# Linear attention and a mixture of experts on one core: the first group's experts woven into the last two rounds of the attention

## The chip, the cores and the metric

The kernel runs on one core of one Trainium2 chip. The metric is the device time of one execution in microseconds (us). The median of three runs stands beside the range of the three.

## What is computed

The input `x` is 4 sequences of 512 tokens with 256 features. Two layers follow, each added to its input and layer-normalised.

```python
x = _layernorm(x + attn(x))     # gated delta rule: 16 key heads, 32 value heads of 128
x = _layernorm(x + ffn(x))

def attn(x):
    mixed = silu(causal_conv(x @ w_qkv, conv_w))      # 4 taps
    q, k, v = split(mixed); z = x @ w_z
    beta = sigmoid(x @ w_b)
    g = -exp(A_log) * softplus(x @ w_a + dt_bias)
    # for each token: S = S*exp(g); S += k (v - k.S)*beta; o = q.S
    return (rmsnorm(o * silu(z)) * norm_gamma) @ w_out

def ffn(x):                      # 8 experts, the best 2 of each token, one shared expert
    h = rmsnorm(x) * rms_weight
    top 2 of softmax(h @ router_w), weights normalised to sum 1
    return sum_e w_e * (silu(h @ w_gate[e]) * (h @ w_up[e])) @ w_down[e] + shared(h)
```

## The kernel before

**Attention.** The work is cut into 64 bodies (16 key heads by 4 sequences; `n` counts them, 0 to 63). A body has 8 cells: 4 chunks of 128 tokens for each of 2 value heads. Within a body the delta rule is solved by blocks: products of the keys (`products`), decays by a scan (`scan`, `m`, `p`), the inverse of a triangular matrix by doubling (steps `join`, `growx`, `growt` at levels 0 to 5, then `newton`, `res`, `finish`, `tt`), and then a recurrence over the 4 chunks: `solve` (TensorE, L1013) -> `u` (ScalarE) -> `write` (TensorE, L1023) -> `s` (VectorE, the new state) -> `read` (TensorE, L1001) -> `rhs` (VectorE) -> the next `solve`. The outputs (`out`, L1039 and L1040) are gated (`og`, VectorE, L1246), squared (`power`, ScalarE), raised to -1/2 and applied (`pow`, `ogs`, GpSimd, L871, L876 and L880), transposed (`turn`, TensorE, L1046) and projected (`project`, L1055) into the accumulator `acc`.

**What sets the order.** There is no scheduler. The table `ORDER` lists for each engine the steps of one round, with the body that each belongs to: in round k a step with ahead 0, 1 or 2 works on body k, k+1 or k+2. `rounds` runs k from -2 to 63 and leaves out bodies that do not exist, so rounds 62 and 63 lack the projections, convolutions and scans of later bodies. Every engine runs its own list strictly in order; semaphores join them. SyncE's queue issues all loads and stores in order.

**Gates.** Before the rounds, and between the first steps of round -2, the decays and betas of all bodies are made in `gates_vector`, `gates_scalar`, `decays_scalar`, `decays_tensor`. GpSimd meanwhile fills the tile `N` with six copies of the identity (`fill_n`, L780). `gall` (VectorE, L335) is what the three matmuls L409 wait for. `decays_scalar` takes exponentials, copies the two row tiles (L374) that are stored to DRAM and loaded back by all bodies, and takes three more exponentials (L377); then ScalarE loads the table for Silu and runs `silu` (L1093) and the second `tap` (L1080).

**Experts.** 4 groups (one sequence each) of 9 experts (8 routed, one shared), i = 0 to 35 in all. For each expert TensorE does `into` (two halves; 8 records of 512 columns in the trace, L527), ScalarE a Silu (L598), VectorE the product `gated` (L678), TensorE `outof` (8 records of 256 columns, L565), VectorE `added` (L692). Before a group's experts come its steps, numbered k: 0 (VectorE, residual and statistics, L623 to L611), 1 (GpSimd, a power, L503), 2 (VectorE, normalise, L615), 3 (ScalarE, squares), 4, 5 (a power, L506), 6 (VectorE, scale), 7 (TensorE transposes L541, ScalarE copies), 8 (TensorE, router logits L548; VectorE, top 2), 9 (a power, L510), 10 (VectorE, weights). For group 0 they stand in round 63 by the table `PREPARE`; for the later groups between experts by `AFTER_EXPERT`. The expert weights are loaded once (`s_mw`) over the attention's `xT`, `conv` and `w_kh`; `into` 1 is followed by `outof` 0, and so on, one expert behind.

```python
for name, i, n in rounds(ORDER["tensor"]):
    run(name, i, n)
    if n == BODIES - 1:
        for k in PREPARE["tensor"].get((name, i), ()):
            prepare_tensor(pe, k, 0)
moe_tensor(pe)
```

## Time and profile before

| | us |
|---|---|
| median of 3 runs | 2387.56 (2385.25 to 2388.07) |
| the profiled execution | 2386.43 |
| its span, first to last instruction | 2384.7 |
| TensorE busy in it | 2324.8 (97%) |
| VectorE, ScalarE, GpSimd busy | 1973.6, 1327.8, 1179.1 |
| mean granted TensorE clock | 0.988 of full speed |

The profiled execution took 1.13 us less than the median; 1.7 us of it lie outside its span. Busy time says how long an engine worked, not whether it was waited for. A timeline row gives the start, the time and the group of instructions; the bracket gives the idle time of the engine before it and what ended it.

### The profile page before, as it was taken

How to read it: one execution, taken by the hardware profiler on the slowest of the kernel's cores; microseconds unless marked ns; L12 is line 12 of the kernel's file. 1: busy time of each engine (PE TensorE's matmuls, PEld its weight loads, DVE VectorE, ACT ScalarE, POOL GpSimd, SP SyncE). 2: the span in 40 equal slices, each digit the busy share in tenths (PEclk: the TensorE clock that was granted, in tenths of full speed). 3: DMA queues.
4: the chain of work that ended last, by engine and by line, in shares of the span. 5: the costliest groups of instructions: out<-in, count | busy, mean ns of one | idle time of the engine just before them, and what ended most of it. 6: DMA issues, size and time to landing. Idle time of an engine off the chain costs nothing.

```text
span 2384.7 us, 53886 instructions
## 1 busy us (share of the span) xinstructions
PE 2324.8 (97%) x20046; PEld 1777.4 (75%) x20046; DVE 1973.6 (83%) x3426; ACT 1327.8 (56%) x4125; POOL 1179.1 (49%) x1198
## 2 busy tenths in 40 slices
PE   6899999999999999999999999999999999987998
PEld 3677877777777777777778777777777777775665
DVE  5888888888888888888888888888888888864665
ACT  3565556665556665566655566665566655652110
POOL 3465555555555555555655655555555555541000
PEclk8999999999999999999999999999999999998999
DMA  4011100111111111011111111111010110010000
GB/s 136 28 54 37 48 34 37 45 37 54 36 46 36 47 37 55 29 36 46 37 55 37 46 37 46 37 54 37 28 54 28 54 37 29 27 70 18 18 10 18
DMA packets 32099, 98.46 MB, mean 41 GB/s; under 512 B 4320, under 2 KB 9824, under 8 KB 31584
## 3 DMA queue, kind: packets, MB, share of 16 engines
q1 hardware_dynamic: 31840, 95.02, 11.3%
q8 instruction: 161, 2.64, 0.5%
q14 instruction: 98, 0.80, 0.1%
HBM read 92.39 MB, written 2.62 MB: 40 GB/s over the span
## 4 chain that ended last, share of the span: by engine, by line
PE 76%; POOL 11%; issue 8%; DVE 3%; ACT 1%; POOLq 0%; DMA 0%; SPq 0%; DVEq 0%; ACTq 0%
PE bank L915 15%; PE bank L939 8%; PE bank L1055 8%; PE bank L952 5%; PE bank L527 4%; PE bank L1013 4%; PE bank L1040 4%; PE bank L962 3%; PE bank L972 3%; PE bank L1001 3%; PE bank L1023 3%; PE bank L1039 3%; PE bank L1046 2%; PE bank L565 2%; PE bank L978 2%
## 5 line engine op out<-in xcount | busy, mean ns | idle before, releaser
L1173 DVE SCALAR_TENSOR_TENSOR conv<-bank,cw_all,conv 128x511 f32<-128x511 f32 (+2 forms) x768 | 565.9, 744 | 16.4 <-ACT conv L1080 7.2
L915 PE MATMUL bank<-xT,w_kh 128*128 128x512 f32 x1024 | 548.5, 618 | 2.3 <-ACT sqj L1102 2.3
L1209 DVE TENSOR_TENSOR N<-bank,lev 128x512 f16<-128x512 f32 x384 | 261.9, 682 | 163.5 <-PE bank L962 163.5
L844 POOL TENSOR_SCALAR_AFFINE_SELECT mhiT<-m32T 128x512 f16<-128x512 f32 x128 | 78.9, 638 | 490.3 <-DVE m32T L1185 490.3
L1125 ACT ACTIVATE X<-bank 128x512 f16<-128x512 f32 x384 | 227.9, 594 | 162.7 <-PE bank L972 157.3
L1080 ACT ACTIVATE conv<-bank,cw_all 128x512 f32<-128x512 f32 x256 | 176.0, 687 | 206.1 <-PE bank L915 206.1
L1055 PE MATMUL bank<-wo,ogT 128*128 128x256 f32 x1024 | 279.8, 396 | 0.0
L939 PE MATMUL bank<-w_kh,xT 128*128 128x256 f32 x1024 | 271.5, 388 | 0.5 <-ACT vals L1115 0.5
L1121 ACT ACTIVATE zs<-bank 128x512 f32<-128x512 f32 x128 | 76.5, 597 | 288.3 <-PE bank L939 288.3
L972 PEld LDWEIGHTS bank<-N,XT 128*128 128x128 f16 x3072 | 122.9, 98 | 127.9 <-DVE N L1209 109.3
L871 POOL TENSOR_TENSOR ms<-ms,epsq 128x8 f32<-128x8 f32 x64 | 12.7, 199 | 406.5 <-ACT og L1140 406.5
L1040 PE MATMUL bank<-U,pT 128*128 128x128 f32 x1024 | 188.8, 277 | 0.0
L939 PEld LDWEIGHTS bank<-w_kh,xT 128*128 128x128 f32 x1024 | 176.1, 192 | 14.8 <-ACT vals L1115 0.7
L962 PEld LDWEIGHTS bank<-X,mhiT 128*128 128x128 f16 x3072 | 137.7, 98 | 66.3 <-issue 20.9
L1055 PEld LDWEIGHTS bank<-wo,ogT 128*128 128x128 f32 x1024 | 176.4, 192 | 13.7
L915 PEld LDWEIGHTS bank<-xT,w_kh 128*128 128x128 f32 x1024 | 155.4, 191 | 17.8 <-ACT sqj L1102 4.0
L972 PE MATMUL bank<-N,XT 128*128 128x64 f16 x3072 | 155.1, 193 | 6.7 <-DVE N L1209 6.7
L1179 DVE TENSOR_TENSOR_SCAN decb<-egb,decb 128x512 f32<-128x512 f32 x128 | 155.6, 1216 | 5.6 <-POOL decb L822 5.6
L1040 PEld LDWEIGHTS bank<-U,pT 128*128 128x128 f32 x1024 | 156.7, 193 | 3.4
L1203 DVE STREAM_TRANSPOSE XT<-X 128x1024 f16<-128x1024 f16 x128 | 158.0, 1235 | 0.7 <-ACT X L1125 0.7
L1140 ACT ACTIVATE og<-og 128x128 f32<-128x128 f32 x512 | 151.0, 298 | 10.9 <-DVE og L1246 5.4
L962 PE MATMUL bank<-X,mhiT 128*128 128x64 f16 x3072 | 154.1, 193 | 2.7 <-ACT X L1125 2.1
(163 smaller groups left out, 5605.1 us busy)
## 6 DMA issues: line engine op xcount, KB each, us to landing
egb<-rows SPq DMA_DIRECT2D x64, 512.0 KB, 3.7
ecb<-rows SPq DMA_DIRECT2D x64, 512.0 KB, 3.7
w_kh<-w_heads SPq DMA_DIRECT2D x16, 768.0 KB, 6.0
wo_raw<-w_out SPq DMA_DIRECT2D x16, 256.0 KB, 6.3
xT<-x_cols SPq DMA_DIRECT2D x4, 512.0 KB, 5.6
qT<-x_rows SPq DMA_DIRECT2D x4, 512.0 KB, 3.5
xT<-gate_up SPq DMA_DIRECT2D x1, 2048.0 KB, 8.1
out<-og SPq DMA_DIRECT2D x4, 512.0 KB, 2.9
```

Of the source, the lines that this page charges most:

```text
L915: mm = pe.matmul(PB[j % 2][:, :], w[:, k, g * P:(g + 1) * P], xT[:, k, b * SEQ:(b + 1) * SEQ], start=(k == 0), stop=(k == KT - 1))
L939: mm = pe.matmul(PB[h][:, 256 * c:256 * c + 256], xT[:, k, t * P:(t + 1) * P], w[:, k, 512:768], start=(k == 0), stop=(k == KT - 1))
L962: mm = pe.matmul(IB[1 - i % 2][:, x * 64:(x + 1) * 64], mhiT[:, x, :], blocks(X[:, x:x + 1, :], i, 0), start=True, stop=True)
L972: mm = pe.matmul(IB[i % 2][:, x * 64:(x + 1) * 64], XT[:, x, :], blocks(N[:, i, x:x + 1, :], i, 0), start=True, stop=True)
L1040: mm = pe.matmul(dst, pT[:, p, x, :], U[:, x, :], start=(c == 0), stop=True)
L1055: mm = pe.matmul(OB[h][:, 256 * c:256 * c + 256], ogT[:, 2 * i + v, :], wo[:, head % 2, v, :], start=(v == 0), stop=(v == VH - 1))
L1080: act.activation(conv[:, g, :], PB[i % 2][:, :], ACT.Copy, scale=cw_all[:, head, g * TAPS + 3:g * TAPS + 4]).then_inc(s_tap, 1)
L1125: act.activation(blocks(X[:, :, :], i, 0), packed(IB[i % 2], i), ACT.Copy).then_inc(s_x, 1)
L1173: dve.scalar_tensor_tensor(conv[:, g, m:], PB[j % 2][:, 0:SEQ - m], cw_all[:, head, g * TAPS + 3 - m:g * TAPS + 4 - m], conv[:, g, m:], op ...
L1179: dve.tensor_tensor_scan(d, egb[:, p, 512 * i:512 * i + 512], d, 0.0, ALU.mult, ALU.add).then_inc(s_scan, 1)
L1203: dve.transpose(flat(XT), flat(X)).then_inc(s_xv, 1)
L1209: dve.tensor_tensor(blocks(N[:, i], i, 0), packed(IB[1 - i % 2], i), blocks(lev[:, 1 + i:2 + i, :], i, 0).broadcast_to(shape), ALU.mult).t ...
```

## The change

It has five parts.

1. The experts of group 0 and its steps move into rounds 61 to 63. A function `drain` on each engine runs a step behind a named step of a named body: step 0 on VectorE behind `join 2` of body 62 (round 61), 1 on GpSimd behind `qe` of body 62 (round 61), 2 behind `scan 0` of body 63 (round 61), 3 to 9 in round 62, 10 and the experts 0 to 5 (`into`), 0 and 1 (`outof`) in round 63.
2. `outof` follows `into` by four experts (`LAG`), where it followed by one. `into` alternates between the PSUM pairs P0, P1 and I0, I1, `outof` writes R0, R1, and four buffers `aT` take the place of two.
3. Buffers: the rows `xg` and the scaled rows `hrow` share `ecb`'s first half, `aT` takes `decb` and `ecb`'s second half, the squares go to parts of `qT` and `kT`. The load of group 0's rows waits for `qe` of body 62 alone.
4. The steps of group 1 come earlier (steps 0 and 2 between round 63's steps, then one expert apart), those of groups 2 and 3 one step an expert from the second on. The statistics of the last norm follow `added` of a group's last expert, and the norm itself the start of the next.
5. At the start: the exponentials L377 stand ahead of the row copies, these behind the first Silu (`rows_scalar`), and GpSimd begins `fill_n` only when `gall` is made (`s_gates` at 12).

```diff
             act.activation(eg_col, gall, ACT.Exp).then_inc(s_gact, 1)
             act.wait_ge(s_cum, 1)
             act.activation(ec_col, bank[2][:, :], ACT.Exp).then_inc(s_gact, 1)
+            for i, what in enumerate((Q_EG, Q_KEYS, Q_EEND)):
+                act.wait_ge(s_cum, i + 1)
+                act.activation(scalars_of(what), bank[2 + i][:, :].rearrange("p (n x) -> p n x", x=CELLS),
+                               ACT.Exp).then_inc(s_gact, 1)
+
+        def rows_scalar(act):
             act.wait_ge(s_rowz, 1)
             for i, skip in enumerate((1, 0)):
                 act.wait_ge(s_rowp, i + 1)
                 act.activation(row_t[i][:, :, skip:], bank4(bank[5 + i])[:, :, skip:], ACT.Copy).then_inc(s_row, 1)
-            for i, what in enumerate((Q_EG, Q_KEYS, Q_EEND)):
-                act.wait_ge(s_cum, i + 1)
-                act.activation(scalars_of(what), bank[2 + i][:, :].rearrange("p (n x) -> p n x", x=CELLS),
-                               ACT.Exp).then_inc(s_gact, 1)
 
         def gates_tensor(pe):
             pe.wait_ge(s_wab, 16)
...
 
-        xg = wide(qT)
+        xg = ecb[:, 0].rearrange("p (c n) -> p c n", n=D)
         x1 = [egb[:, i].rearrange("p (c n) -> p c n", n=D) for i in range(2)]
-        hrow = wide(m32T)
-        sqx = wide(keys[:, 0])
+        hrow = xg
+        sqx = [t[:, 256 * i:256 * i + 256] for t in (qT[:, 0], kT[:, 1]) for i in range(2)]
         hT = [wide(t, SEQ) for t in (vT, rhs)]
         sg = wide(TT[:, 0], SEQ)[:, 0:2]
-        aT = wide(U, SEQ)[:, 0:2]
+        aT = ([wide(decb, SEQ)[:, i] for i in range(2)]
+              + [ecb[:, 1].rearrange("p (i n) -> p i n", n=SEQ)[:, i] for i in range(2)])
         y = wide(qE[:, 0])
         outrow = wide(og)
         bn = sb("bn", [P, 2, CH, 6])
@@ -458,22 +461,14 @@
...
         def moe_loads(sp):
 
-            sp.wait_ge(s_kq, 2 * BODIES)
-            sp.wait_ge(s_ktp, 2 * BODIES)
-            sp.wait_ge(s_qe, BODIES)
+            sp.wait_ge(s_qe, BODIES - 1)
...
 
-                sp.wait_ge(s_ln1, g * NORM)
+                sp.wait_ge(s_htp, g)
...
+            def last(g):
                 pool.wait_ge(s_ln2, g * NORM + 2 * CH + 1)
                 pool.tensor_tensor(st1[:, 1, 1, :], st1[:, 1, 0, :], expo[:, 0:1].broadcast_to([P, CH]), ALU.pow).then_inc(s_pw2, 1)
 
-        def into(pe, g, e):
-            i = g * NX + e
-
-            for a, dst in enumerate(((I0, I1), (R0, R1))[i % 2]):
-                if i > 1:
+            for k in (1, 5, 9):
+                prepare_pool(pool, k, 1)
+            for g in range(2, B):
+                prepare_pool(pool, 1, g)
+                last(g - 2)
+                for k in (5, 9):
+                    prepare_pool(pool, k, g)
+            for g in range(B - 2, B):
+                last(g)
+
+        def into(pe, i, a):
+            if a == 0:
+                if i == 0:
+                    pe.wait_ge(s_mw, 64)
+                    pe.wait_ge(s_rt, 1)
+                elif i == 1:
+                    pe.wait_ge(s_new, 2 * BODIES)
+                else:
                     pe.wait_ge(s_a, i - 1)
-                for k in range(KT):
-                    mm = pe.matmul(dst[:, :], gate_up_of(e)[:, k, a * P:(a + 1) * P], hT[g % 2][:, k, :],
-                                   start=(k == 0), stop=(k == KT - 1))
-                mm.then_inc(s_gup, 1)
...
+        def outof(pe, i):
+            if i == 0:
+                pe.wait_ge(s_u, 4 * BODIES)
+            pe.wait_ge(s_a, i + 1)
+            for h, dst in enumerate(OUTOF):
+                if i > 0:
+                    pe.wait_ge(s_y, (i - 1) * CH + 2 * h + 2)
+                for c in range(2):
+                    mm = pe.matmul(dst[:, 256 * c:256 * c + 256], aT[i % 4][:, (2 * h + c) * P:(2 * h + c + 1) * P],
+                                   down_of(i % NX), start=True, stop=True)
+                mm.then_inc(s_dnp, 1)
...
+            for i in range(DRAINED, B * NX):
+                outof(pe, i - LAG)
+                for a in range(2):
+                    into(pe, i, a)
+                g, e = divmod(i, NX)
+                if g + 1 < B and e == (7 if g == 0 else 5):
+                    prepare_tensor(pe, 7, g + 1)
+                if g + 1 < B and e == (8 if g == 0 else 6):
+                    prepare_tensor(pe, 8, g + 1)
+            for i in range(B * NX - LAG, B * NX):
+                outof(pe, i)
```

```diff
@@ vector, experts: behind the named steps, then one loop @@
+        def gated(dve, i):
+            if i == 2:
+                dve.wait_ge(s_qe, BODIES)
+            dve.wait_ge(s_sg, i + 1)
...
+            def drain(name, i, n):
+                if (name, i, n) == ("join", 2, BODIES - 2):
+                    prepare_vector(dve, 0, 0)
+                elif (name, i, n) == ("scan", 0, BODIES - 1):
+                    prepare_vector(dve, 2, 0)
+                elif (name, i, n) == ("tt", 1, BODIES - 2):
+                    prepare_vector(dve, 4, 0)
+                elif (name, i, n) == ("rhs", 3, BODIES - 2):
+                    prepare_vector(dve, 6, 0)
+                elif (name, i, n) == ("join", 4, BODIES - 1):
+                    prepare_vector(dve, 8, 0)
+                elif (name, i, n) == ("tt", 1, BODIES - 1):
+                    prepare_vector(dve, 10, 0)
...
+                elif (name, i, n) == ("og", 1, BODIES - 1):
+                    added(dve, 0)
+                    gated(dve, 4)
+                    prepare_vector(dve, 0, 1)
+                    added(dve, 1)
+                    gated(dve, 5)
+                    prepare_vector(dve, 2, 1)
@@ pool @@
+            pool.wait_ge(s_gates, 12)
             fill_n()
             scale_wo(0)
             for name, i, n in rounds(ORDER["pool"]):
                 run(name, i, n)
+                if (name, i, n) == ("qe", 0, BODIES - 2):
+                    prepare_pool(pool, 1, 0)
+                elif (name, i, n) == ("diag", 0, BODIES - 1):
+                    prepare_pool(pool, 5, 0)
+                elif (name, i, n) == ("ogs", 1, BODIES - 2):
+                    prepare_pool(pool, 9, 0)
```

How rows move on three engines. **GpSimd, from `qe` of body 62 on** (round 61). Before:

```order
L837 TENSOR_TENSOR qE<-qT,ecb 128x768
L871 TENSOR_TENSOR ms<-ms,epsq 128x8
L876 TENSOR_TENSOR ms<-ms,expo 128x8
L880 TENSOR_TENSOR og<-og,ms 128x512 x2
L798 TENSOR_SCALAR ss<-ssum 128x4
L803 TENSOR_TENSOR nr<-ss,expk 128x8
```

After the change:

```order
L855 TENSOR_TENSOR qE<-qT,ecb 128x768
L498 TENSOR_TENSOR st<-st,expo 128x4
L886 TENSOR_TENSOR ms<-ms,epsq 128x8
L891 TENSOR_TENSOR ms<-ms,expo 128x8
L895 TENSOR_TENSOR og<-og,ms 128x512 x2
L816 TENSOR_SCALAR ss<-ssum 128x4
L821 TENSOR_TENSOR nr<-ss,expk 128x8
```

The power of step 1 (L498 now) stands between `qE` and the three rows of `pow` and `ogs` of body 61, on which `turn` waits.

**VectorE, from the turned block `XT` of body 62 on** (round 61). Before:

```order
L1203 STREAM_TRANSPOSE XT<-X 128x1024
L1209 TENSOR_TENSOR N<-bank,lev 128x64x8
L1209 TENSOR_TENSOR N<-bank,lev 128x32x16
L1173 SCALAR_TENSOR_TENSOR conv<-bank,cw_all,conv 128x511
L1173 SCALAR_TENSOR_TENSOR conv<-bank,cw_all,conv 128x510
L1209 TENSOR_TENSOR N<-bank,lev 128x16x32
```

After the change:

```order
L1271 STREAM_TRANSPOSE XT<-X 128x1024
L1277 TENSOR_TENSOR N<-bank,lev 128x64x8
L632 TENSOR_TENSOR ecb<-ecb,acc 128x1024
L617 BN_STATS bn<-ecb 128x6 x4
L620 BN_AGGR mv<-bn 128x2 x4
L622 TENSOR_SCALAR st<-mv 128x4
L1277 TENSOR_TENSOR N<-bank,lev 128x32x16
L1241 SCALAR_TENSOR_TENSOR conv<-bank,cw_all,conv 128x511
L1241 SCALAR_TENSOR_TENSOR conv<-bank,cw_all,conv 128x510
L1277 TENSOR_TENSOR N<-bank,lev 128x16x32
```

The four kinds of rows of step 0 stand between the levels 2 and 3 of the doubling (`N`).

**TensorE, round 63, from `finish` on.** Before (L997 `finish`, L1013 `solve`, L1023 `write`, L1001 `read`, L1040 `out`):

```order
L997 MATMUL bank<-XT,mloT 128x128 x8
L1013 MATMUL bank<-vals,TT 128x128 x2
L1023 MATMUL bank<-U,keys 128x128 x2
L1001 MATMUL bank<-S,kT 128x256
L1040 MATMUL bank<-U,pT 128x128 x2
L1013 MATMUL bank<-rhs,TT 128x128 x2
L1023 MATMUL bank<-U,keys 128x128 x2
```

After the change (L532 is `into`; L1017 `finish`, L1033 `solve`, L1043 `write`, L1021 `read`, L1060 `out`):

```order
L532 MATMUL bank<-vT,xT 128x512 x2
L1017 MATMUL bank<-XT,mloT 128x128 x8
L532 MATMUL bank<-vT,xT 128x512 x2
L1033 MATMUL bank<-vals,TT 128x128 x2
L532 MATMUL bank<-vT,xT 128x512 x2
L1043 MATMUL bank<-U,keys 128x128 x2
L532 MATMUL bank<-vT,xT 128x512 x2
L1021 MATMUL bank<-S,kT 128x256
L1060 MATMUL bank<-U,pT 128x128 x2
L1033 MATMUL bank<-rhs,TT 128x128 x2
L532 MATMUL bank<-vT,xT 128x512 x2
L1043 MATMUL bank<-U,keys 128x128 x2
```

A half of an `into` (2 matmuls, which the trace shows as 4 records of 512 columns) stands ahead of nearly every step of the recurrence.

## Rows read from the trace of the kernel before

**Rows 1.** Busy time by stretches: stretch, length, five engines (records), granted clock, DMA

```profile
2130.00:2140.00 10.00, 8.95 (x106) 7.77 (x105) 2.54 (x4) 4.45 (x8) 3.40 (x3) 0.67 0.49 198
2141.00:2163.70 22.70, 15.50 (x87) 12.51 (x85) 10.19 (x28) 2.83 (x13) 1.01 (x1) 0.78 0.00 1
```

**Rows 2.** Timeline, last turn, TensorE: start us, us, engine, line, operation, [idle before, releaser]

```profile
2141.01 0.22 PE L989 MATMUL bank<-X,mhiT 128*128 128x128 f16 x1
...
2157.43 1.22 PE L1001 MATMUL bank<-S,kT 128*128 128x256 f32 x2 [2.72 <-DVE S L1239]
...
2171.83 2.12 PE L1046 MATMUL bank<-tri_sb,og 128*128 128x128 f32 x8 [8.10 <-POOL og L880]
...
2181.69 7.11 PE L527 MATMUL bank<-vT,xT 128*128 128x512 f32 x16
2188.64 1.89 PE L565 MATMUL bank<-conv,U 128*128 128x256 f32 x8
2190.37 3.60 PE L527 MATMUL bank<-vT,xT 128*128 128x512 f32 x8
...
2374.16 1.97 PE L565 MATMUL bank<-w_kh,U 128*128 128x256 f32 x8 [0.20 <-DVE qE L692]
```

**Rows 3.** Timeline, gates at the start, all engines

```profile
16.24 7.71 POOL L780 COPY N<-identh 128x1024 f16<-128x1024 f16 x6 [11.84 <-DMA rms_sb<-rms_w]
...
17.05 0.77 DVE L325 SCALAR_TENSOR_TENSOR pT<-pT 128x512 f32<-128x512 f32 x1
...
17.75 1.52 DVE L326 SCALAR_TENSOR_TENSOR TT<-pT 128x512 f32<-128x512 f32 x1
...
21.24 0.63 ACT L364 ACTIVATE U<-TT 128x512 f32<-128x512 f32 x1
...
22.98 1.52 DVE L333 SCALAR_TENSOR_TENSOR U<-pT,U 128x512 f32<-128x512 f32 x1
...
24.53 1.41 DVE L335 SCALAR_TENSOR_TENSOR TT<-U 128x512 f32<-128x512 f32 x1
...
26.09 5.08 PE L409 MATMUL bank<-TT,tri_sb 128*128 128x512 f32 x6 [6.30 <-DVE TT L335]
```

**Rows 4.** Timeline, from the row copies to the second tap, ScalarE

```profile
31.70 1.08 ACT L374 ACTIVATE ogT<-bank 128x508 f32<-128x508 f32 x2 [2.94 <-PE bank L412]
32.67 1.58 ACT L377 ACTIVATE sc_all<-bank 128x512 f32<-128x512 f32 x3
34.27 1.28 ACT L1093 ACT_TABLE_LOAD   x1
...
36.10 0.67 ACT L1080 ACTIVATE conv<-bank,cw_all 128x512 f32<-128x512 f32 x1
```

**Rows 5.** Timeline, round 61, VectorE, GpSimd and TensorE

```profile
2099.74 0.69 DVE L1209 TENSOR_TENSOR N<-bank,lev 128x512 f16<-128x512 f32 x1 [2.05 <-PE bank L962]
...
2097.35 0.20 POOL L871 TENSOR_TENSOR ms<-ms,epsq 128x8 f32<-128x8 f32 x1 [6.46 <-ACT og L1140]
...
2099.35 2.04 POOL L880 TENSOR_TENSOR og<-og,ms 128x512 f32<-128x512 f32 x2
...
2100.74 0.63 PE L1046 MATMUL bank<-tri_sb,og 128*128 128x128 f32 x4
```

**Rows 6.** Timeline, group 0's first steps, VectorE and GpSimd

```profile
2153.72 1.21 DVE L623 TENSOR_TENSOR qT<-qT,acc 128x1024 f32<-128x1024 f32 x1
...
2164.38 1.37 DVE L615 TENSOR_SCALAR egb<-qT,mv,st 128x256 f32<-128x256 f32 x4
...
2156.94 1.01 POOL L503 TENSOR_TENSOR st<-st,expo 128x4 f32<-128x4 f32 x1 [23.46 <-DVE st L611]
```

**Rows 7.** Timeline, round 62, VectorE and TensorE

```profile
2127.36 0.69 DVE L1246 TENSOR_TENSOR og<-bank,zs 128x512 f32<-128x512 f32 x1 [2.37 <-PE bank L1040]
...
2129.83 0.61 PE L972 MATMUL bank<-N,XT 128*128 128x64 f16 x8 [2.28 <-DVE N L1209]
...
2132.94 1.09 PE L1046 MATMUL bank<-tri_sb,og 128*128 128x128 f32 x4
```

More of the change, by code:

```diff
@@ new lines, in moe_pool @@
+            for g in range(2, B):
[13 more added lines that the diff above has]
+                else:
+                    pe.wait_ge(s_a, i - 1)
+            for k in range(KT):
+                mm = pe.matmul(INTO[i % 2][a][:, :], gate_up_of(i % NX)[:, k, a * P:(a + 1) * P], hT[i // NX % 2][:, k, :],
+                               start=(k == 0), stop=(k == KT - 1))
+            mm.then_inc(s_gup, 1)
@@ new lines, in last_norm @@
+        def last_norm(dve, g):
+            dve.wait_ge(s_pw2, g + 1)
+            if g > 0:
+                dve.wait_ge(s_out, 16 * g)
+            normalise(dve, 1, outrow, y, s_ln2)
+        def moe_vector(dve):
+            for i in range(DRAINED, B * NX + LAG):
+                j = i - LAG
+                if j % NX == 0 and j > 0:
+                    last_norm(dve, j // NX - 1)
+                added(dve, j)
+                if i < B * NX:
+                    gated(dve, i)
+                    g, e = divmod(i, NX)
+                    if g + 1 < B:
+                        if e == (6 if g == 0 else 1):
+                            prepare_vector(dve, 0, g + 1) if g > 0 else prepare_vector(dve, 4, g + 1)
+                        if e == (7 if g == 0 else 2):
+                            prepare_vector(dve, 2, g + 1) if g > 0 else prepare_vector(dve, 6, g + 1)
+                        if g > 0 and e == 3:
+                            prepare_vector(dve, 4, g + 1)
+                        if g > 0 and e == 4:
+                            prepare_vector(dve, 6, g + 1)
+                        if e == (8 if g == 0 else 6):
+                            prepare_vector(dve, 8, g + 1)
+                        if g > 0 and e == 8:
+                            prepare_vector(dve, 10, g + 1)
+                    if g == 1 and e == 0:
+                        prepare_vector(dve, 10, 1)
+            last_norm(dve, B - 1)
@@ L1058, in run @@
                         mm.then_inc(s_opp, 1)
+            def drain(name, i, n):
+                if n < BODIES - 1:
+                    return
+                if (name, i) == ("join", 2):
+                    prepare_tensor(pe, 7, 0)
+                elif (name, i) == ("join", 3):
+                    prepare_tensor(pe, 8, 0)
+                elif (name, i) == ("newton", 1):
+                    into(pe, 0, 0)
+                elif (name, i) == ("finish", 1):
+                    into(pe, 0, 1)
+                elif (name, i) == ("solve", 0):
+                    into(pe, 1, 0)
+                elif (name, i) == ("write", 0):
+                    into(pe, 1, 1)
+                elif (name, i) == ("solve", 1):
+                    into(pe, 2, 0)
+                elif (name, i) == ("write", 1):
+                    into(pe, 2, 1)
+                elif (name, i) == ("solve", 2):
+                    into(pe, 3, 0)
+                elif (name, i) == ("write", 2):
+                    into(pe, 3, 1)
+                elif (name, i) == ("out", 3):
+                    outof(pe, 0)
+                    into(pe, 4, 0)
+                    into(pe, 4, 1)
+                elif (name, i) == ("turn", 1):
+                    outof(pe, 1)
+                    into(pe, 5, 0)
+                    into(pe, 5, 1)
             for name, i, n in rounds(ORDER["tensor"]):
@@ L1063, in _ @@
                     decays_tensor(pe)
[L1064 to L1066 removed]
+                drain(name, i, n)
             moe_tensor(pe)
@@ L1151, in _ @@
                     decays_scalar(act)
-                if n == BODIES - 1:
-                    for k in PREPARE["scalar"].get((name, i), ()):
-                        prepare_scalar(act, k, 0)
+                if n == 0 and (name, i) == ("silu", 0):
+                    rows_scalar(act)
+                drain(name, i, n)
             moe_scalar(act)
```

190 lines of the change are left out of this document (80 added, 110 removed).

## The prediction

> **What bounds the kernel now.** I read the page first: TensorE is busy for 97% of the span, so nearly all rounds are closed to a change like this one. Then the windows and the timeline of TensorE at the two ends, where the busy share falls. The windows show the last round [rows 1]: in the 22.7 us from 2141.0 TensorE is busy for 15.5 us, at a mean granted clock of 0.78. The timeline says why [rows 2]: a serial recurrence runs alone, each step waits for VectorE or ScalarE (2.72 us before the third `read`, where group 0's step 0 sits in VectorE's queue), and then TensorE stands 8.10 us for GpSimd's `ogs`. From the start of `newton` at 2141.01 to the first expert at 2181.69 are 40.7 us. From there on TensorE is dense: two `into` in 6.95 us (2181.69 to 2188.64), 3.43 each, and 1.73 for an `outof` (2188.64 to 2190.37). The steady expert loop hence has no wait for the lag of four to remove, and I cost part 2 at nothing there. The chain of waits agrees: almost only TensorE from 2171 on.
>
> At the start TensorE waits 6.30 us for `gall` [rows 3], and then for ScalarE's list [rows 4].
>
> **Part 5, the start.** GpSimd's six copies run from 16.24 to 23.95 [rows 3]. The VectorE instructions beside them that read two SBUF tiles of 512 columns take 1.52 us (L326, L333; L335 1.41, beside the next GpSimd instruction), while the first (L325) took 0.77. Without the copies the path is: L326 done 0.75 earlier, so the logarithm starts at 20.5 and ends at 21.1 (L364 has 0.63); L333 starts at 21.15 where it started at 22.98, takes 0.77, L335 the same, and L409 starts at 22.75 where it started at 26.09: 3.3 us. Then ScalarE: before, from the end of L409 at about 31.0 it waited for transposes, made the row copies (31.70, 1.08), the exponentials (1.58) and the table load (1.28), and began the second `tap` at 36.10, 5.1 us on. Now two of the three exponentials are made while L409 still runs, and what follows its end is 0.2 + 0.53 + 1.28 + 0.63 (Silu) + 1.08 (the copies, now behind it) = 3.7 us [rows 4]. That is 1.3 more, 4.6 in all; I take **-4.5**, since the rounds follow as a chain of taps, convolutions and loads. The stored rows come out only 1 us earlier, but they have many convolutions' time until the first scan reads them.
>
> A rule bears on the copies' new place. The Trainium skill ("SBUF — State Buffer", Who interferes with whom) says that a VectorE instruction with two SBUF inputs contends with a GpSimd instruction that reads SBUF, which the 1.52 us agree with and L325's 0.77, inside GpSimd's span, does not. By that rule the copies now meet the two such instructions of `betas_vector`, 0.75 us more for each. By the trace alone any VectorE instruction of those 7.7 us may be slowed. The sum stays at -4.5 if the second `tap`, at 31.6, still comes last, and would be -3 if the slower list did. The gain has bounds of 2.5 (that, and nothing from the new order on ScalarE) and 6 (L409's six records also out of the low clock).
>
> **Round 61, step 0 and the power behind it.** VectorE is free from 2097.69 to 2099.74 (2.05 idle before level 3) [rows 5]. Step 0 takes 3.2 us (2153.72 to GpSimd's start at 2156.94) [rows 6]. Put at 2097.7 it ends at 2100.9, so level 3 is 1.1 us late. What hurts more stands on GpSimd. Its power of step 1 now stands ahead of `pow` of body 61, and waits for step 0: 2100.9 + 1.01 = 2101.9 [rows 6]. `pow` started at 2097.35 before, and its first `ogs` ended at 2100.4 (half of 2.04 from 2099.35), 3.05 later; now 2101.95 + 3.05 = 2105.0. TensorE's `turn`, at 2100.74 before, starts at 2105.1 [rows 5]. TensorE's list is in order, and all of its later steps stand behind `turn`: **+4.4**, which holds the 1.1. ScalarE's `tap` 3 stands behind the copy of `turn`, so the last convolutions are as late. GpSimd's `kn` and `diag` of body 63 end at about 2110.5, just ahead of the scan's new time of 2110.7. The load of the rows is issued when `qe` of body 62 ends, before GpSimd's idle 6.46 us that end at 2097.35 [rows 5], and so has landed by 2097.7: nothing.
>
> An idle time of this kind costs clock as well. In round 62 TensorE idled 2.28 us at 2127.5 [rows 7], and the window from 2130 shows a granted clock of 0.67 [rows 1], that is 6.6 of 10 us at the lower of the two levels (1.2 for 2.4 GHz); four transposes take 1.09 us there [rows 7] and 0.63 in round 61 [rows 5]. My idle time is 3.2 us. 6.6 us at half speed lose at most 3.3 us, of which waits hide some. I take **+2.0**, bounds 0 and 3.5.
>
> **Round 61, step 2.** 1.37 us [rows 6] on VectorE between the scan and `res`, where it is idle for 0.2: **+1.2**; bounds 0 and 1.4.
>
> **Round 62.** Steps 4 and 5 lie in waits. Step 6 (1.1 us) lies in the 2.37 us before `og` and step 7's transposes (1.0) in TensorE's idle 2.28 [rows 7]; with that gap half filled the lower clock behind it may not come, which gives back up to 2. Against it stand the router's 16 records of step 8, 1.7 us at 0.11 each, in a wait that I take to be half as long: +0.9. I take **-0.5**, bounds -2 and +2.
>
> **Round 63 and the experts.** The round's own work up to `out 3` at full clock: a record's time goes by its columns, 0.43 us for 512 (3.43 for 8, rows 2), so 0.11 for 128; with 87 records [rows 1] 9.3 us. (15.5 us busy at 0.78 would be 12.1; it counts modelled ends that denser work covers.) With `into` 0 to 3 (4 x 3.43 = 13.7) ahead of the steps, each 1.72 us half covers the wait of about 0.5 of `solve` -> `u` -> `write` or `write` -> `s` -> `read`. Uncovered stay `read` -> `rhs` -> `solve`, 0.7 in all. `out 3` ends 9.3 + 13.7 + 0.7 = 23.7 us from `newton`. VectorE has three instruction groups in such a chunk's 4.3 us or more, `s`, `gated` and `rhs`, none of which works on more than 512 columns: no queue. From there to `turn` are `og`, `power`, `pow`, `ogs`: 5.6 us from `og`'s start to `turn` in round 62 [rows 7], of which TensorE was itself late by 0.4. `outof` 0 and `into` 4 (5.2) cover all but 0.2; the second `turn` follows a GpSimd half later, 30.5. `outof` 1, `into` 5 and the projection (16 records of 256 columns, 3.5) end at 39.2. Before, the same work and group 0's steps took 40.7 us, and the six `into` and two `outof` would take another 6 x 3.43 + 2 x 1.73 = 24.0. The gain is 64.7 - 39.2 = 25.5.
>
> Two new waits go off it. Step 7 of group 1 on TensorE stands right behind `into` 7, and step 6, which it needs, on VectorE behind `gated` 7 (0.9 after `into` 7 ends, first row 0.3 later): 1.2 us. At the end four `outof` follow each other on one pair of banks, where each waits for `added`: the row at 2374.16 has 0.20 idle [rows 2], and three such waits, 0.6, against one before: 0.5. **-23.8**; bounds -18 and -26.
>
> **The sum** is made against the profiled execution, 2386.4 us, of which the trace spans 2384.7: -4.5 + 4.4 + 2.0 + 1.2 - 0.5 - 23.8 = -21.2, so 2365.2. The median of the runs is 1.1 above that execution, and I forecast **2366.3 us**.
>
> **Rivals.** *The last round gives less.* The halves of `into` lengthen the recurrence: if their 13.7 us are added to a recurrence that keeps half of its 7.2 us of idle, and a lower clock returns once, the round gives 17 and not 23.8: 2373. For it speaks that three engines must meet at each chunk in a fixed order; against it that every product sits at least one half `into` behind what it needs.
>
> *The start gives nothing*: the rounds begin by something else, as the stored rows or GpSimd's copies ahead of `kn`. 2371. Against it: the copies end by 32, and the steps that need GpSimd come behind the second `tap`.
>
> *GpSimd's wait is cheap*: VectorE finishes step 0 in other gaps, or the clock stays up. Then +7.6 becomes about +1: 2360. Against it stands the strict order of the list.
>
> *Slower than before*: after round 61's idle time TensorE's clock stays at the lower level through rounds 61 to 63. Each us of dense work there takes twice as long as at full clock, so a stretch of t us loses t/2; it eats the 21.2 when it lasts 42 us more than I allow. Over the 60 us up to the end of `out 3` it would lose 30: 2396. In the trace the one such stretch, after 2.28 us of idle time, had ended within the 10 us [rows 1], with dense work; hence a small chance.
>
> *The change doesn't do what it says*: the experts might still run behind the round, if `into` 0 had to wait there for the weights. Their load needs only the projections and gates of body 63, which end in round 62, most of a round before `newton`. I put this with the first rival.
>
> **How the numbers follow.** Forecast within its own bounds 0.50, last round less 0.18, start nothing 0.12, cheap wait 0.15, slower 0.03, and 0.02 for a sum of losses that ends near no change. The cases other than the last two lie between 2358 and 2376, and this range leaves out about 2 in 10. No change means within 0.2% (4.8 us), about what a measurement of this kernel can tell: faster 0.95, same 0.02, slower 0.03.
>
> **What would show it.** The start of L409's successor near 22.8 us and the first scan near 44.5. GpSimd's `pow` of body 61 right behind the power of step 1, with an idle time of 3 us on TensorE ahead of `turn` in round 61 and none elsewhere in it; the granted clock behind it. In round 63 TensorE busy from `newton` to `out 3` in about 24 us, and less than 1 us of idle time before `turn`, where 8.1 stood. From there to the end the same 5.16 us an expert. I am wrong if round 61 keeps its length, if idle time before `write` and `read` stays in round 63, or if the expert loop has waits of its own.

## The result, and the profile after

The changed kernel takes **2362.8 us** (median of 4 runs, 2362.24 to 2363.48); before, 2387.3 us (4 runs). The ratio is 0.9901, 95% interval 0.9886 to 0.9915, so the gain of 1.0% is clear of noise. The forecast was 2366.3, range 2358 to 2376. The profiled span went from 2384.7 to 2361.0 us: 23.7 us.

The page, busy time by engine:

```profile
span 2361.0 us, 53889 instructions
...
PE 2315.4 (98%) x20046; PEld 1770.2 (75%) x20046; DVE 1968.3 (83%) x3426; ACT 1327.7 (56%) x4125; POOL 1178.8 (50%) x1198
```

**The start** (timeline of GpSimd, VectorE, TensorE and ScalarE, answering to [rows 3, 4]; first three more lines of the kernel before):

```profile
14.96 0.68 DVE L316 COPY zs<-bank 64x512 f32<-64x512 f32 x1 [2.75 <-PE bank L386]
...
20.37 1.25 DVE L330 TENSOR_SCALAR rhs<-TT 128x512 f32<-128x512 f32 x1
...
31.00 0.60 PE L412 MATMUL bank<-tri_sb,og 128*128 128x128 f32 x4
```

```profile
14.60 0.68 DVE L316 COPY zs<-bank 64x512 f32<-64x512 f32 x1 [2.75 <-PE bank L388]
...
17.30 0.68 DVE L326 SCALAR_TENSOR_TENSOR TT<-pT 128x512 f32<-128x512 f32 x1
...
19.03 0.42 DVE L330 TENSOR_SCALAR rhs<-TT 128x512 f32<-128x512 f32 x1
...
21.35 0.69 DVE L335 SCALAR_TENSOR_TENSOR TT<-U 128x512 f32<-128x512 f32 x1
...
27.56 1.15 DVE L340 SCALAR_TENSOR_TENSOR sc_all<-rhs 128x512 f32<-128x512 f32 x1
...
22.21 5.96 POOL L798 COPY N<-identh 128x1024 f16<-128x1024 f16 x6 [17.81 <-DVE TT L335]
...
22.19 4.51 PE L411 MATMUL bank<-TT,tri_sb 128*128 128x512 f32 x6 [2.76 <-DVE TT L335]
26.53 0.60 PE L414 MATMUL bank<-tri_sb,og 128*128 128x128 f32 x4
...
30.13 0.69 ACT L1130 ACTIVATE conv<-bank,cw_all 128x512 f32<-128x512 f32 x1
```

Without GpSimd's copies beside them the gates' instructions take 0.7 and 0.4 us where they took 1.5 and 1.25; `gall` is ready 3.9 us earlier, the second `tap` 6.0 us (36.10 to 30.13), and the first scan stands at 42.00 where it stood at 49.00. From round 12 to round 60 all is 7.5 us earlier. L340 and L344 now take 1.15 and 1.41 us where both took 0.69: L340 runs beside the last of the copies, L344 beside the GpSimd product that follows them (L804, from 28.21). In this trace neither is on the path, since VectorE waits another 0.70 us for `tap` behind them.

**Round 61** (timeline of GpSimd, then TensorE, answering to [rows 5], and the windows):

```profile
2093.30 1.02 POOL L498 TENSOR_TENSOR st<-st,expo 128x4 f32<-128x4 f32 x1 [9.92 <-DVE st L622]
2094.29 0.20 POOL L886 TENSOR_TENSOR ms<-ms,epsq 128x8 f32<-128x8 f32 x1
2094.57 1.64 POOL L891 TENSOR_TENSOR ms<-ms,expo 128x8 f32<-128x8 f32 x1
2096.28 2.04 POOL L895 TENSOR_TENSOR og<-og,ms 128x512 f32<-128x512 f32 x2
...
2093.87 0.41 PE L992 MATMUL bank<-N,XT 128*128 128x64 f16 x8 [0.74 <-DVE N L1277]
2097.38 0.66 PE L1066 MATMUL bank<-tri_sb,og 128*128 128x128 f32 x4 [3.11 <-POOL og L895]
...
2099.29 1.91 PE L1075 MATMUL bank<-wo,ogT 128*128 128x256 f32 x4
```

```profile
2090.00:2110.00 20.00, 15.25 (x155) 11.74 (x155) 14.28 (x30) 10.72 (x31) 9.00 (x10) 0.91 0.00 1
2130.00:2140.00 10.00, 9.84 (x111) 8.93 (x112) 3.90 (x19) 4.60 (x10) 3.52 (x4) 0.83 0.06 19
2141.20:2164.20 23.00, 22.56 (x107) 14.12 (x105) 10.65 (x30) 5.09 (x16) 0.00 (x0) 1.00 0.01 1
```

The power of step 1 (L498) waits for step 0 and keeps `pow` (L886) behind it; `turn` waits 3.11 us. Set against the 7.5 us gained, `turn` is 4.2 us late and the first `newton` 5.6; behind `turn` the clock is low (four `project` records took 1.91 us, where four at full clock take 1.1). The end of VectorE's step 2 adds 1.0. The third window answers to [rows 1]: 22.56 of 23.0 us busy at clock 1.00, where it was 15.5 of 22.7 at 0.78.

**The last round and the experts** (timeline of TensorE, answering to [rows 2]):

```profile
2141.23 1.94 PE L532 MATMUL bank<-vT,xT 128*128 128x512 f32 x4
...
2161.74 0.75 PE L1033 MATMUL bank<-rhs,TT 128*128 128x128 f32 x4 [0.44 <-DVE rhs L1295]
...
2164.11 1.89 PE L544 MATMUL bank<-conv,decb 128*128 128x256 f32 x8
...
2170.48 0.66 PE L1066 MATMUL bank<-tri_sb,og 128*128 128x128 f32 x4 [0.34 <-POOL og L895]
...
2179.59 1.89 PE L544 MATMUL bank<-conv,ecb 128*128 128x256 f32 x8
...
2191.26 1.14 PE L559 MATMUL bank<-tri_sb,ecb 128*128 128x128 f32 x8 [1.19 <-DVE ecb L647]
...
2350.24 1.97 PE L544 MATMUL bank<-w_kh,ecb 128*128 128x256 f32 x8 [0.20 <-DVE qE L701]
```

`newton` of this round starts at 2140.34. `out 3` ends 23.8 us on, `outof` 2 starts 39.25 us on (forecast 23.7 and 39.2). Of the 8.10 us before `turn` 0.34 is left, before the second half of it. What is new is the wait of 1.19 us before step 7 of group 1, and three of 0.20 in the tail.

### The profile page after: what moved, and what is told of

Its sections match the earlier page's. It is cut to its first block, busy times and chain, and to the rows that moved or that the text cites. A ratio compares the mean times of both kernels' runs of the same rounds, so it can differ in the third digit from the quotient of the medians.

```text
span 2361.0 us, 53889 instructions
## 1 busy us (share of the span) xinstructions
PE 2315.4 (98%) x20046; PEld 1770.2 (75%) x20046; DVE 1968.3 (83%) x3426; ACT 1327.7 (56%) x4125; POOL 1178.8 (50%) x1198
## 4 chain that ended last, share of the span: by engine, by line
PE 73%; POOL 12%; issue 10%; DVE 3%; ACT 1%; POOLq 0%; DMA 0%; SPq 0%; DVEq 0%
PE bank L935 15%; PE bank L959 8%; PE bank L1075 7%; PE bank L972 4%; PE bank L1033 4%; PE bank L532 4%; PE bank L1060 3%; PE bank L982 3%; PE bank L992 3%; PE bank L1021 3%; PE bank L1043 3%; PE bank L1059 3%; PE bank L544 2%; PE bank L1066 2%; PE bank L998 2%
## 5 line engine op out<-in xcount | busy, mean ns | idle before, releaser
L886 POOL TENSOR_TENSOR ms<-ms,epsq 128x8 f32<-128x8 f32 x64 | 12.8, 200 | 428.6 <-ACT og L1190 428.6
L1060 PE MATMUL bank<-U,pT 128*128 128x128 f32 x1024 | 187.3, 275 | 0.0
L1060 PEld LDWEIGHTS bank<-U,pT 128*128 128x128 f32 x1024 | 155.2, 192 | 3.3
```

The costliest lines, as they stand in the source:

```text
L1060: mm = pe.matmul(dst, pT[:, p, x, :], U[:, x, :], start=(c == 0), stop=True)
```

## The experiments

Executions of one kernel scatter by up to 6.7 us (where, see the last section), so each kernel is also read in two pieces of its one trace: up to the second scan of body 62 (2078.61 before, 2071.09 changed), which holds the start, and from there to the end (306.1 before, 289.9 changed), which holds the rest of the change. The changed kernel run again (`changed_again`) gave 2363.7 us (2363.3 to 2365.1; the slowest is 2.3 above the expected 2362.8) and 289.9 for the second piece.

The second piece is not free of scatter either. In the two kernels of the next experiment it has the code of the kernel before, and yet it took 303.8 and 303.9 us, not 306.1. The difference lies in the last round, which from the start of `newton` to the first expert took 38.15 and 38.23 us there and 40.68 before. TensorE was idle for 15.3 us of it in all three traces, but the granted clock differed. The stretch of [rows 1] in `start_alone`:

```profile
2134.66:2155.30 20.64, 13.43 (x87) 10.90 (x85) 10.20 (x28) 2.81 (x13) 1.01 (x1) 0.92 0.00 1
```

The same 87 records took 20.6 us at 0.92 and 22.7 us at 0.78. A difference of up to 2.3 us between two second pieces can therefore be the clock of that execution, and is shown only where rows show it.

> The changed kernel once more, unedited, to stand beside the other kernels of this set on the same chip and to see how its runs scatter: 2362.8 us, within 1 us.

**The start alone, and its first half alone.** The kernel before with

```
+            pool.wait_ge(s_gates, 12)          # both kernels
             fill_n()
...
+        def rows_scalar(act):                  # start_alone only, with the rest of part 5 on ScalarE
```

> The kernel before with part 5 alone (GpSimd waits for the gates, ScalarE makes all exponentials ahead of the two row copies). Theory A, from the traces of both kernels: everything from round 12 on stands 7.5 us earlier, and that is all part 5's: 2387.3 - 7.5 = 2379.8 us, with TensorE's first L409 near 22.2 and the first scan near 42.0. Theory B, my forecast: 4.5 us, 2382.8, and the other 3 us come from somewhere else in the change. Theory C: the rounds begin by something else, 2387.

> The kernel before with GpSimd's wait for the gates alone; ScalarE keeps its old list (row copies ahead of the exponentials). Theory A: the gates' VectorE chain gives 3.9 us, and the order on ScalarE gives the remaining 3: about 2383. Theory B: the whole of part 5 is the contention between GpSimd's copies and VectorE, and the order on ScalarE is worth nothing: the same time as with both edits, near 2380. The VectorE instructions of the gates that took 1.52 and 1.25 us should take 0.7 and 0.4 under both.

Measured: 2379.55 us with both (8 runs; ratio 0.9972, 0.9961 to 0.9983) and 2382.51 with GpSimd's wait alone (11 runs; 0.9982, 0.9973 to 0.9991), against 2386.37 before. That is 6.8 and 3.9 us. The difference of 3 for the order on ScalarE isn't firm, as the intervals of the two meet. The traces say how. ScalarE, wait alone and then both:

```profile
27.20 1.08 ACT L374 ACTIVATE ogT<-bank 128x508 f32<-128x508 f32 x2 [3.07 <-PE bank L412]
...
31.60 0.67 ACT L1081 ACTIVATE conv<-bank,cw_all 128x512 f32<-128x512 f32 x1
```

```profile
28.18 1.06 ACT L380 ACTIVATE ogT<-bank 128x508 f32<-128x508 f32 x2
29.13 0.69 ACT L1083 ACTIVATE conv<-bank,cw_all 128x512 f32<-128x512 f32 x1
```

With the old list ScalarE waits 3.07 us for the row transposes and has all of the exponentials, the table load and Silu behind it; with the new one `tap` comes 2.5 us earlier, and the first scan stands at 41.2 and not 44.5. The rows place the gain as follows.

- **GpSimd's wait.** From the start of L316 on VectorE to the first product of `gall` on TensorE it is 11.1 us before, and 7.6 in both kernels and in the changed one: 3.5 us.
- **The order on ScalarE.** From the first row transpose (L412, now L414) to the second `tap` it is 5.1 us before and with the wait alone, and 3.6 in `start_alone` and in the changed kernel: 1.5 us.
- **Between `tap` and the first scan** it is 12.9 us before and with the wait alone, 12.1 in `start_alone`, 11.9 to 12.2 in most of the changed kernels' traces, and 13.0 in that of the combined kernel below. No run shows what makes these 0.7 to 1.0 us.
- **The rest is scatter.** The six products of `gall` took 5.08 us before, 4.51 with the wait alone and 2.81 in `start_alone`, at a granted clock of 0.69, 0.81 and 1.00 between 20 and 30 us. By the second scan of body 62, `start_alone` is 6.6 us ahead of the kernel before and the wait alone 1.9. Ten traces with the whole of part 5 and nothing added to the start are 3.5 to 7.5 us ahead (middle 6.4), and the changed kernel's 7.5 is the largest.

So the start is worth 6 to 7 us. Theory A's time fits, C is out, and B's 2382.8 us lies above all eight runs; the wait gives 3.5 and the order 1.5 by rows.

**GpSimd's power behind `pow`.** The changed kernel with

```
-                if (name, i, n) == ("qe", 0, BODIES - 2):
+                if (name, i, n) == ("diag", 0, BODIES - 1):      # power_behind_pow
+                if (name, i, n) == ("ogs", 1, BODIES - 3):       # power_behind_ogs
                     prepare_pool(pool, 1, 0)
```

> The changed kernel with one edit: GpSimd's power of step 1 stands behind the diag of body 63, and no longer ahead of pow of body 61. Theory A: the strict order of GpSimd's list makes the idle time of 3.1 us ahead of turn in round 61 and the low clock behind it (1.5 us); both go, some 0.5 us of it stays as join 3 waits for step 0 on VectorE: 2362.8 - 5 = 2358 us, granted clock 1.0 from 2095 to 2105. Theory B: VectorE's step 0 (3.2 us) is what makes round 61 late, through level 3 and the convolutions, and GpSimd is only seen waiting: less than 1.5 us, 2361.5 or more.

> The changed kernel with GpSimd's power of step 1 behind ogs of body 61 (the last experiment on it had it behind the diag of body 63; its profiled execution was 3.5 us shorter than that of the changed kernel, but its other runs were not). Theory A: the idle time ahead of turn in round 61 is gone and the list's order was its cause; the time saved there comes back in some executions as a lower clock at another place, since the executions differ in their mean granted clock (0.992 to 0.995): 2359 to 2364 us, a scatter of over 3 us, and the longer executions have the lower clock. Theory B: the idle time costs nothing, something later in round 62 waits as long: 2362.8 us with a scatter of 1 us, and newton of round 62 at the same time as in the changed kernel.

Medians 2362.96 (2359.2 to 2364.0) and 2364.14 us (2359.0 to 2364.6): no gain to be seen over the changed kernel's. But the second piece is 285.9 and 286.1 us, 3.8 to 4.0 shorter in each trace. GpSimd, VectorE and TensorE in round 61 of the first:

```profile
2090.61 2.70 POOL L891 TENSOR_TENSOR ms<-ms,expo 128x8 f32<-128x8 f32 x1
...
2093.55 0.90 DVE L622 TENSOR_SCALAR st<-mv 128x4 f32<-128x4 f32 x1
...
2095.09 0.41 PE L991 MATMUL bank<-N,XT 128*128 128x64 f16 x8 [1.47 <-DVE N L1276]
2095.34 0.63 PE L1065 MATMUL bank<-tri_sb,og 128*128 128x128 f32 x4
```

`turn` waits for nothing, and the granted clock of this stretch is 1.00. A wait of 1.47 us (0.74 in the changed kernel) stands before level 3: `pow` and step 0 now run side by side, and each slows the other (`pow` 2.70 for 1.64, the step's last instruction 0.90 for 0.17). So theory A's cause is shown: the order of the list made the wait, and taking it away gives 4 us in the trace, not 5. The medians, though, are what theory B forecast for `power_behind_pow` (2361.5 or more), and just above A's range for `power_behind_ogs`. The profiled execution was the fastest of four both times, and the others lie 2.7 to 5.7 us above it. Those of `power_behind_ogs` have the lower mean clock (0.992 for 0.994), as theory A has it there, but `power_behind_pow` has one at 0.995 that is 2.7 us longer. Where they lose the time no trace shows.

**The experts behind the recurrence.** `into` 0 to 3 stand behind `out 3`, and their gates and products with them:

```
-                elif (name, i) == ("newton", 1):
-                    into(pe, 0, 0)
...
                 elif (name, i) == ("out", 3):
+                    for j in range(4):
+                        into(pe, j, 0)
+                        into(pe, j, 1)
                     outof(pe, 0)
```

> The changed kernel, but into 0 to 3 with their gates and products stand together behind out 3, not between the steps of the recurrence (outof 0, into 4 and all the rest as before). Theory A: the recurrence runs alone in about 19.5 us from newton to out 3 (22.7 less the wait for step 0, which is now made earlier), the four into follow in 13.7, and the second turn is reached some 9 us later than in the changed kernel; its clock is lower as well: 2362.8 + 9 to 11 = 2372 to 2374. Theory B: most of the last round's gain came from the group's steps being made earlier and from the filled wait of 8.1 us, and the places between the recurrence's steps are worth little: 2363 to 2366.

2373.93 us (2372.2 to 2376.5; ratio 0.9948), 11.1 above the changed kernel; the second piece is 9.4 longer. TensorE's waits between 2141 and 2200, and the line of `into`:

```profile
PE bank L1043 <- ACT U L1170: 1.4, 3, 0.5
PE bank L1021 <- DVE S L1287: 1.4, 2, 0.7
PE bank L1033 <- DVE TT L1267: 0.8, 1, 0.8
...
2162.38 13.90 PE L532 MATMUL bank<-vT,xT 128*128 128x512 f32 x32
```

Alone, the recurrence takes 19.6 us at a clock of 0.84 to 0.87 and waits at each step; then come the 13.7. Theory A. The places between the steps hence hold 9 of the last round's 23 us. What remains is the filled wait before `turn` and group 0's steps made earlier (the wait before the third `read` was 2.72 us, here it is 0.70); how the other 14 us divide between the two isn't measured.

**The lag of four.** In the main loop `outof` follows `into` by one expert, on VectorE too (shortened; step 1 and the last norm on GpSimd change places with it):

```
+            for j in range(DRAINED - LAG, DRAINED - 1):
+                outof(pe, j)
             for i in range(DRAINED, B * NX):
-                outof(pe, i - LAG)
                 for a in range(2):
                     into(pe, i, a)
+                outof(pe, i - 1)
```

> The changed kernel with part 2 undone in the main loop: from expert 6 on outof follows into by one expert and not by four (outof 2, 3 and 4 are made in a row first). Theory A: the lag is worth nothing once TensorE is dense; the three outof in a row move their waits on VectorE from the end of the kernel to the place behind expert 5 (0.43 us each in both), and the last outof waits for its product instead: 2362 to 2364 us, 5.16 us an expert. Theory B: a lag of one exposes the wait for Silu and the product in each expert, 0.3 us or more for each of 30: 2371 us or more.

2365.12 us (2364.05 to 2367.96), and 290.6 us for the second piece, 0.7 longer. The waits are nearly those of the changed kernel, 1.3 before step 7 and three of 0.20, of which two now stand behind expert 5. There is no wait in the loop, and theory B is excluded. The time is 1 us above theory A's range and 1.4 above `changed_again`, with the scatters overlapping; part 2 is worth about 1 us at most.

**Two edits behind the last round.** The lines of TensorE (shortened; steps 7, 8 and 10 move with them on ScalarE and VectorE):

```
-                for a in range(2):
-                    into(pe, i, a)
+                if i == 9:
+                    prepare_tensor(pe, 8, 1)
+                into(pe, i, 0)
+                if i == 8:
+                    prepare_tensor(pe, 7, 1)
+                into(pe, i, 1)
...
+        def pair_of(i):
+            return (O0, O1) if i > B * NX - LAG and i % 2 else OUTOF
```

> The changed kernel with two edits behind the last round: step 7 of group 1 stands between the halves of into 8 (and step 8 ahead of into 9), and the last four outof take two pairs of banks in turn. Theory A: the wait of 1.19 us before step 7 goes, and the last three outof start 1.73 us apart and not 2.16: 2362.8 - 1.2 - 1.3 = 2360.3 us. Theory B: VectorE's sums (1.74 us a piece) set the end, not the banks, so only the first edit counts: 2361.6 us.

2363.54 us (2362.4 to 2365.8): by the runs, not to be told from the changed kernel; the second piece is 1.65 shorter. TensorE and VectorE:

```profile
2194.68 1.04 PE L565 MATMUL bank<-tri_sb,ecb 128*128 128x128 f32 x8
...
2215.56 1.97 PE L550 MATMUL bank<-w_kh,decb 128*128 128x256 f32 x8 [0.86 <-DVE qE L711]
...
2345.86 5.19 DVE L711 SCALAR_TENSOR_TENSOR qE<-bank,wd,qE 128x256 f32<-128x256 f32 x12
```

Both edits do what was meant (the wait of 1.19 is gone, and VectorE's last sums run without a pause, 1.3 us shorter), but two steps of VectorE now stand in one expert, and a new wait of 0.86 takes part of it back: 1.19 + 1.3 - 0.86 = 1.6. That is theory A but for the new wait, by the rows; B is out, as VectorE's sums did move closer, though the median lies above both theories' times.

**All of them together.** The power behind `ogs`, both edits above, and

```
+                        if i == 11:
+                            prepare_vector(dve, 10, 1)
```

> The changed kernel with the edits whose traces were shorter: GpSimd's power of step 1 behind ogs of body 61, step 7 of group 1 between the halves of into 8, the last four outof on two pairs of banks, and step 10 of group 1 one expert later (where the last set's trace shows a new wait of 0.86 us on VectorE's pile of two steps). Theory A: the terms add, 4.5 to 5 us for round 61 where the clock allows it, 1.2 and 1.3 behind: the profiled span near 2354.8 us, the median 2361.5 if most executions lose some 5 us to a lower clock in the last rounds as power_behind_ogs did, 2356.5 if not. Theory B: the edits behind the last round are hidden by the output's transfers: median as power_behind_ogs, 2364.

**2357.17 us** (2355.2 to 2361.8; ratio 0.9874, 0.9857 to 0.9890), 5.6 below the changed kernel. The parts' traces gave 3.9 and 1.65, and the wait of 0.86, which is gone from this trace, would make it 6.4. The terms add within the scatter, as theory A has it. All four executions lie below the changed kernel's eight, though the two intervals meet. The profiled execution was the slowest of the four, and even so its second piece is 285.0 us, 4.9 below the changed kernel's, at a clock of 0.66 between 2130 and 2140; in its round 61 `turn` waits for nothing, as in the two traces above.

**Idle time filled with unread products.**

```
+            def fill(times, rhs):
+                for _ in range(times):
+                    pe.matmul(bank[7][:, :], ident, rhs, start=True, stop=True)
```

> The combined kernel with five products of 512 columns that nobody reads, put into TensorE's two idle times of rounds 61 and 62 (three ahead of growx 3 of body 62, where 1.5 us were idle, two ahead of growx 2 of body 63, where 1.4 us were; each product takes 0.43 us). Theory A: the executions that are some 5 us longer lose it because TensorE's clock falls behind these idle times; filled, the granted clock stays up, the scatter closes, and the median comes down to the profiled time, about 2357 us. Theory B: the longer executions lose their time elsewhere (the start, whose clock differs between traces), and the fill changes nothing or costs up to 0.5 us: the same median and scatter as the combined kernel.

> The last kernel with the start filled too: unread products of 512 columns in TensorE's idle times of round 0 (six ahead of the wait for gall, three before the transposes of kT, five before proj 4, nine before the transposes of vT). Theory A: the clock of 0.67 to 0.83 between 20 and 50 us is what idle time leaves behind; filled, it is near 1.0, the six L411 take 2.8 us and not 4.5, and the kernel is 2 to 3 us faster than without this fill. Theory B: the start waits for ScalarE and VectorE whatever TensorE's clock, and the fill gives nothing, or costs up to 1 us where it holds up a product that was ready.

> The kernel with both fills again, cut to the idle times: the last traces show that an unread product of 512 columns takes 0.86 us (two records of 0.43), twice what I had reckoned, so that the fills were longer than the idle times and held TensorE up by some 4 to 5 us at the start and 1.4 us in rounds 61 and 62. Now three products (2.6 us) in the 2.76 us before gall, two in 1.76, two in 2.41, four in 3.8, one each in rounds 61 and 62. Theory A: what varies between executions of one kernel is the clock of the start (1.0, 0.83 or 0.66 between 30 and 50 us in the traces so far); with the start filled the transposes of vT begin near 42 us as in the best traces, the scatter is under 2 us, and the median is 2355 us, 2 below the combined kernel's. Theory B: the fills cost as much as the clock gives, since each is TensorE work that holds up what becomes ready early: 2357 us or more.

2357.94 us (2356.8 to 2359.4), 2361.85 (2360.4 to 2362.0) and 2357.51 (2353.0 to 2358.3). In the second kernel, of TensorE:

```profile
19.61 5.31 PE L1127 MATMUL bank<-xT,tri_sb 128*128 128x512 f32 x12
24.77 2.74 PE L411 MATMUL bank<-TT,tri_sb 128*128 128x512 f32 x6
...
40.00:50.00 10.00, 9.51 (x30) 4.83 (x29) 5.52 (x7) 2.78 (x5) 0.00 (x0) 1.00 0.73 270
```

The first kernel, filled in rounds 61 and 62 alone, has the combined kernel's median and a second piece of 284.4 us for 285.0; theory B fits, but for its scatter of 2.6 us where the combined kernel had 6.7. In the second kernel the fill keeps the clock at 1.00 from 20 to 50 us, where the combined kernel's trace has 1.00, 0.66 and 0.66 in the three windows (its six L411 took 2.81 us unfilled). But an unread product took 0.86 us and not 0.43, my fills were twice too long, and the first scan came at 43.3. Its scatter was 1.6 us, and it was 4 us slower than the first. Cut to size, the first scan came at 41.2, the earliest of the changed kernels, and yet the second scan of body 62 stands at 2073.2, no earlier than in those without a fill at the start (2071.1 to 2075.1). In rounds 61 and 62 the single products left a second piece of 281.8 us, 3.2 shorter than the combined kernel's, at a clock of 1.00 where that had 0.66. The median is the combined kernel's. So filling the start gains nothing that shows, although its clock rises; for the last rounds one trace says 3 us, and four runs don't show it. With the fills cut to size the scatter is 5.3 us: theory A fell there.

## Why the prediction was right, and what was mis-sized

By its terms, forecast against the trace: start -4.5, measured **-7.5**; `turn`'s wait +4.4, +4.2; low clock +2.0, +1.5; step 2 +1.2, +1.0; round 62 -0.5, +0.2; last round and experts -23.8, -23.0. Sum -21.2, measured -23.7 (the rounded terms give -23.6). These are differences of two traces, and two of them are scatter in part: the start's, and the last round's, whose 40.7 us before were 38.2 in two other traces of the same code. Against those the last round gives 20.5 us.

- **Start, the term that was mis-sized.** Forecast 4.5 with a bound of 6; 6.8 by the runs of `start_alone` (4.1 to 9.3 by its interval), 7.5 in the changed kernel's trace. The two steps that were worked out were right: the 3.3 us for GpSimd's copies measured 3.5, and the 3.7 us from the end of L409 to the second `tap` measured 3.6. What failed is that the sum stopped at the second `tap`. L409's six records came out of the low clock in part (5.08 to 4.51 us, which only the bound allowed for), the first scan gained another 1.0 us behind `tap`, and 0.36 us came ahead of any edit, by chance. The last 0.5 us lie between the first scan and body 2, where the same code scatters by 3.5.
- **Round 61.** The mechanism, its place and its size were as forecast, and taking it away gives back 4 of the 6.7 us; the rest is VectorE's step 0 and 2. The rival "GpSimd's wait is cheap" is out.
- **Round 62.** The clock between 2130 and 2140 rose from 0.67 to 0.83 as hoped, the router's 16 records took 1.93 us, and both together gave nothing.
- **Last round.** 23.8 us to the end of `out 3`, 39.25 to `outof` 2, the new waits 1.2 and 0.6: as forecast. The new time of the stretch was forecast to 0.1 us; the gain of 23 is set against an execution whose last round had a low clock. The rival "gives less" is out; with the experts behind the recurrence the kernel took 11.1 us longer, 9.4 of them in the second piece.
- **Contention.** The rule of the Trainium skill ("SBUF — State Buffer", Who interferes with whom) put the copies' new victims at L340 and L344. By that rule, the trace agrees: 1.15 us beside the copies and 1.41 beside the product behind them, for 0.7. In the changed kernel the list of ScalarE, not they, was last, as the sum assumed. In the traces of `start_alone` and of the combined kernel they were: the convolution starts right behind L344, some 0.95 us after `tap` ended.
- "The start gives nothing", "clock stays low through 63" and "experts wait for weights" are out: `into` 0 starts right behind `newton`, and the clock is 1.00 in the window behind it.

## What to carry to other kernels

When a dense engine has one thin stretch, independent work in halves between the steps of the serial chain fills it. The gain can exceed the stretch's idle time (here 15.3 us idle in 40.7, and a gain of 20.5 to 23), since the busy time of a thin stretch was spent at a lower clock too. Whatever is moved early takes a place in every in-order list it touches: look there for the instruction behind it that somebody waits for (here a power of 1 us that cost 4 in the trace). And where a small instruction of one engine waits for another's, order the list by when inputs come, as ScalarE's exponentials ahead of the row copies show (1.5 us).

## What the runs showed that I had not expected

**Where one kernel's executions differ.** The scans of bodies 0 and 2 in the changed and in the combined kernel, and their windows:

```profile
42.00 2.33 DVE L1247 TENSOR_TENSOR_SCAN decb<-egb,decb 128x512 f32<-128x512 f32 x2
...
109.76 1.21 DVE L1247 TENSOR_TENSOR_SCAN decb<-egb,decb 128x512 f32<-128x512 f32 x1
...
40.00:50.00 10.00, 6.97 (x34) 5.65 (x35) 5.72 (x8) 3.32 (x7) 0.62 (x2) 0.83 0.51 197
...
70.00:80.00 10.00, 8.89 (x80) 8.14 (x81) 7.58 (x11) 4.32 (x10) 0.70 (x2) 0.83 0.06 19
```

```profile
42.12 2.33 DVE L1259 TENSOR_TENSOR_SCAN decb<-egb,decb 128x512 f32<-128x512 f32 x2
...
113.37 1.22 DVE L1259 TENSOR_TENSOR_SCAN decb<-egb,decb 128x512 f32<-128x512 f32 x1
...
40.00:50.00 10.00, 7.00 (x31) 5.92 (x32) 4.86 (x6) 3.25 (x7) 0.00 (x0) 0.66 0.42 167
...
70.00:80.00 10.00, 7.46 (x77) 6.68 (x78) 7.07 (x10) 4.48 (x9) 0.00 (x0) 0.66 0.01 2
```

The code up to here is the same, and the first scan too; at body 2 the combined kernel is 3.5 us behind, with a lower granted clock on the way. From there to body 62 all traces agree within 0.7 us (1961.3 and 1961.8 here). The Trainium skill ("TensorE: Matmul & The Clock Gate", Part 1) says that the number of matmuls at the lower clock differs from run to run of one kernel; by that, the traces agree, and here it is worth 3.5 us, more than most single edits. That the clock makes these 3.5 us is read from two windows and not forced by a run. A second place is the last round, with 2.3 us between traces of the same code. A piece of the trace, counted from a fixed instruction, takes the first place out of a comparison, and the rows of an edit say whether it did what was meant; neither replaces more runs.

**Contention in both directions.** A VectorE instruction with one SBUF input was slowed as well (L330: 1.25 for 0.42 us), while the reciprocal beside the same copies kept its 3.34. The Trainium skill ("SBUF — State Buffer", Who interferes with whom) names `tensor_scalar` among the operations that can take the shared ports; by that rule, the trace agrees. And GpSimd's own `pow` was stretched from 1.64 to 2.70 us by VectorE's step 0.
